# FFN token columns at a stride of 124, and a down product with 128 stationary columns

## The chip, the cores and the metric

The kernel runs on one core of a Trainium2 chip. The metric is the device time of one execution in microseconds, lower is better. A slot and a sample, used below, are units of the kernel's own loop.

## What is computed

The input is x of 64 x 55 x 55 x 96 floats. First a depthwise convolution with 25 x 25 taps of which every third counts, multiplied by x, plus a bias, plus x. The result is taken as 64 samples of 3025 tokens of 96 channels. A token mixer follows: layer norm, a product to 192 channels with ReLU, a Fourier transform over the tokens, gates on the real and the imaginary part, the inverse transform, and a product back to 96 channels, added to the tokens. Last comes the FFN, the part that the change touches:

```python
def _qlinear(x, W, b):
    y = q_acc(jnp.einsum('bsk,nk->bsn', q_mul(x), q_mul(W)))
    return q_acc(y + q_mul(b))
...
h = jax.nn.relu(_qlinear(x, W1, b1))      # 96 -> 384
y = _qlinear(h, W2, b2)                   # 384 -> 96
...
t = t + _L1_ffn_ref(_ln_t(t), W1, b1, W2, b2)
```

`q_mul` rounds to an 8-bit float with 5 exponent and 2 mantissa bits, `q_acc` to a 16-bit float with 5 and 10.

## The kernel before

There are two stages. `conv_stage` (lines 170 to 344) does the convolution and writes to DRAM. `mixer_stage` (from line 347) first sets up weights and constants in a block of its own (lines 440 to 567, with the clearing of buffers at lines 540 to 546), and then runs everything else as one software pipeline.

The 3025 tokens of a sample are 121 x 25: 121 (`U`) on the partitions, 25 (`S`) columns. A sample is cut into eight chunks of columns, the first of 4 and seven of 3 (`CHUNK`). So there are 512 chunks, and the pipeline's loop counter g, a slot, runs from -9 to 555. In each slot every engine does one piece of each step, each for another chunk: a step with offset k works on chunk g - k. The order in a slot is written out by hand, one loop to an engine (TensorE lines 1137 to 1161, ScalarE 855 to 881, VectorE 990 to 1010, GpSimd 750 to 759, the DMA queue of SyncE 693 to 710), and semaphores connect them.

TensorE in slot g: `columns` (line 1021, the second forward transform), `rows` part 1 (1046), `widen` part 0 (1033), `mix` (1061, 1062), `rows` part 0 (1046), `inverse` (1073), `down` (1085), `turn` (1098), `widen` part 1 (1033), `inverse_rows` (1122), `up` (1111), `turn2` (1133). `rows` part 1 waits, through the bank that they share, for VectorE's `residual` (line 985, writes `t2`), which waits for the `inverse_rows` of the slot before.

The FFN of a chunk with w columns (3 or 4) goes through these steps:

- `normalise` (VectorE, 961) writes the normalised tokens in fp8 and `turn2` turns them, with an output of 121 columns for each token column, 128 apart in PSUM
- `out_turn2` (ScalarE, 768) copies them to `xq`, fp8, 96 partitions, with the token columns side by side at a stride of 121
- `up` (TensorE, offset 41): three matmuls (`FM` = 3) with `w1q` stationary, 128 columns, and `xq` moving, 121 w columns, into three banks
- `out_up` (ScalarE, 838) copies the three to `y16`, f16, rows of 484
- `widen_bias` (VectorE, offset 42): three additions of the bias with ReLU on `y16` in place (921), of 121 w elements rounded up to even, and one cast to `hq` in fp8 (927)
- `down` (TensorE, offset 42, same slot): for each token column and each m of three, one load of 121 columns of `hq` as the stationary operand and one matmul with `w2q` moving, 96 columns: 3 w pairs of load and matmul
- `out_down` (ScalarE, 821) and `finish` (GpSimd, 733 and 737): copy, bias, residual, then the DMA to `out`

GpSimd's five operations of a slot are `cut_value` (721), `add_sum` (727), `scale` (747) and `finish` (733, 737); ahead of them it waits for this slot's `normalise`. In slots with g modulo 8 equal to 6, VectorE first computes the layer norms' `variance` (lines 896 to 902) of a whole sample, before `residual`, and at its end `inverse_root` (908 to 912). In slots 1 to 5 it does the statistics of five incoming columns (969).

Of the kernel before, what the change touches and what calls it, by code (L numbers as in the profile page):

```python
# [11 lines left out]
F8 = mybir.dt.float8e5  # L12
# [3 lines left out]
C = 96  # L16
# [3 lines left out]
FM = F // 128  # L20
# [59 lines left out]
U = 121  # L80
# [12 lines left out]
PART = (0, 5, 10, 15, 20, 25)  # L93
JC = 4
KC = 8
TOK = JC * U
AR = 3
XR = 3
OR = 3
# [18 lines left out]
def tokens(n):  # L118
    return CHUNK[n % NS], CHUNK[n % NS + 1]
# [15 lines left out]
def upto(n):  # L135
    return max(0, min(n, CHUNKS))
# [210 lines left out]
def mixer_stage(nc, x1, p, a_d, g_d, out):  # L347
    with ExitStack() as ctx:
        def sb(name, shape, dt=F32):
            return ctx.enter_context(nc.sbuf_tensor(name, shape, dt))  # L350
# [18 lines left out]
        w2q = sb("w2q", [128, FM, C], F8)  # L369
# [20 lines left out]
        xn2 = [sb(f"xn2{s}", [U, JC, C], F8) for s in range(2)]  # L390
        xq = [sb(f"xq{s}", [C, TOK], F8) for s in range(XR)]
        y16 = [sb(f"y16{s}", [128, FM, TOK], F16) for s in range(2)]
        hq = [sb(f"hq{s}", [128, FM, TOK], F8) for s in range(2)]
        z16 = [sb(f"z16{s}", [U, JC, C], F16) for s in range(2)]
        o_sb = [sb(f"o_sb{s}", [U, JC, C]) for s in range(OR)]
        bn = sb("bn", [U, 2 * S, 6])
# [6 lines left out]
        ps = ctx.enter_context(nc.psum_tensor("ps", [128, 8, 512], F32))  # L403


        with ExitStack() as wctx:
# [69 lines left out]
            def _(dve):  # L476
                steps = [0]

                def then(ins):

                    steps[0] += 1
                    ins.then_inc(w_step, 1)
                    dve.wait_ge(w_step, steps[0])

                dve.wait_ge(w_in, 16 * (LOADS - 1))
                last = None
# [5 lines left out]
                for v, n in zip((var1, var2, rows[3], rows2[3]), newton):  # L492
                    last = nc.vector.reciprocal(v, n[1])
                then(last)
                for v, n in zip((var1, var2, rows[3], rows2[3]), newton):
                    last = nc.vector.tensor_tensor(n[1], v, v, ALU.mult)
                then(last)
                for v, n in zip((var1, var2, rows[3], rows2[3]), newton):
                    last = nc.vector.tensor_tensor(n[1], n[1], n[0], ALU.mult)
                then(last)  # L500
                for v, n in zip((var1, var2, rows[3], rows2[3]), newton):
                    last = nc.vector.tensor_scalar(n[1], n[1], -0.5, 1.5, ALU.mult, ALU.add)
                then(last)
                for v, n in zip((var1, var2, rows[3], rows2[3]), newton):
                    last = nc.vector.tensor_tensor(v, v, n[1], ALU.mult)
# [11 lines left out]
                for a in range(2):  # L517
                    last = nc.vector.tensor_scalar(w1n[:, a, :], w1n[:, a, :], gam1[:, a:a + 1], None,
                                                   ALU.subtract)
# [20 lines left out]
                nc.vector.memset(mixed[:, PAIRS_K, :], 0.0)  # L540
                for v in toks:
                    nc.vector.memset(v[:, :, C:C + 1], 1.0)
                for v in y16:
                    nc.vector.memset(v[:, :, :], 0.0)
                then(nc.vector.memset(spec[HH:HH + 1, :, :, :], 0.0))
                nc.vector.memset(spec[HH:HH + 1, 0, 0, 0:1], 1.0)

# [72 lines left out]
        TURNED, WIDE, ROW, MIXP, INVP, DOWNP = 2, 3, 4, 5, 6, 7  # L620
# [141 lines left out]
        def _(act):  # L762
            def out_turn2(n):
                w = tokens(n)[1] - tokens(n)[0]
                act.wait_ge(turned2, n + 1)
                if n >= XR:
                    act.wait_ge(f1_done, n - XR + 1)
                nc.scalar.activation(xq[n % XR][:, 0:w * U].rearrange("p (j t) -> p j t", t=U),
                                     ps[0:C, TURNED, :].rearrange("p (j t) -> p j t", j=JC)[:, 0:w, 0:U],
                                     ACT.Copy, saturate=False).then_inc(xq_ready, 1)  # L770

# [59 lines left out]
                                     ACT.Copy).then_inc(xnt_ready, 1)  # L831

            def out_up(n):
                w = (tokens(n)[1] - tokens(n)[0]) * U
                act.wait_ge(f1_done, n + 1)
                if n >= 2:
                    act.wait_ge(hq_ready, n - 1)
                nc.scalar.activation(y16[n % 2][:, :, 0:w], ps[:, MIXP:MIXP + FM, 0:w],  # L838
                                     ACT.Copy).then_inc(y16_ready, 1)
# [15 lines left out]
            for g in SLOTS_G:  # L855
                if here(g - TURN2 - 1):
                    out_turn2(g - TURN2 - 1)
                if here(g - GATE):
                    gate_value(g - GATE)
                if here(g - 1):  # L860
                    rows_out(g - 1, 1)
                if here(g):
                    relu(g, 0)
                if here(g - GATE):
                    gate_sum(g - GATE)
                if g % NS == 6 and 0 <= (g + 2) // NS < B + 5:
                    root((g + 2) // NS)
                if here(g - MIX):
                    out_mix(g - MIX)
                if here(g):  # L870
                    rows_out(g, 0)
                if here(g - INV):
                    out_inverse(g - INV)
                if here(g - DOWN):
                    out_down(g - DOWN)
                if here(g - TURN):
                    out_turn(g - TURN)
                if here(g):
                    relu(g, 1)
                if here(g - UP):  # L880
                    out_up(g - UP)

        @block.vector
        def _(dve):
# [28 lines left out]
                dve.sem_inc(scale_ready, 1)  # L913

            def widen_bias(n):
                w = (tokens(n)[1] - tokens(n)[0]) * U
                w += w % 2
                y, q = y16[n % 2], hq[n % 2]
                dve.wait_ge(y16_ready, n + 1)
                for m in range(FM):  # L920
                    last = nc.vector.tensor_scalar(y[:, m, 0:w], y[:, m, 0:w], b1q[:, m:m + 1], 0.0,  # L921
                                                   ALU.add, ALU.max)
                last.then_inc(relu_ready, 1)
                if n >= 2:
                    dve.wait_ge(f2_done, n - 1)
                dve.wait_ge(relu_ready, n + 1)
                nc.vector.tensor_copy(q[:, :, 0:w], y[:, :, 0:w], saturate=False).then_inc(hq_ready, 1)  # L927
# [85 lines left out]
        def _(pe):  # L1013
            def columns(t):
                p0, _, n, hf = group(t)
                pe.wait_ge(acol_in[t % NS // 2], 16 * (t // NS + 1))
                if t:
                    pe.wait_ge(v_ready, t)
                    pe.wait_ge(m_ready, t)
                for p in range(n):  # L1020
                    last = nc.tensor.matmul(COL[:, p, 0:Q], acol[:, p0 + p, hf * HH:(hf + 1) * HH],  # L1021
                                            fb[:, p0 + p, :], start=True, stop=True)
                last.then_inc(x_done, 1)
# [53 lines left out]
            def down(n):  # L1077
                w = tokens(n)[1] - tokens(n)[0]
                pe.wait_ge(hq_ready, n + 1)
                pe.wait_ge(y16_ready, n + 1)  # L1080
                if n:
                    pe.wait_ge(z_ready, n)
                for j in range(w):
                    for m in range(FM):
                        last = nc.tensor.matmul(ps[0:U, DOWNP, C * j:C * (j + 1)],  # L1085
                                                hq[n % 2][:, m, j * U:(j + 1) * U], w2q[:, m, :],
                                                start=(m == 0), stop=(m == FM - 1))
                last.then_inc(f2_done, 1)

# [10 lines left out]
                last.then_inc(turned, 1)  # L1100

            def up(n):
                w = (tokens(n)[1] - tokens(n)[0]) * U
                pe.wait_ge(xq_ready, n + 1)
                pe.wait_ge(w2_ready, upto(n + UP - MIX + 1))
                pe.wait_ge(g_ready, upto(n + UP - INV + 1))
                if n:
                    pe.wait_ge(z_ready, n)
                    pe.wait_ge(y16_ready, n)
                for m in range(FM):  # L1110
                    last = nc.tensor.matmul(ps[:, MIXP + m, 0:w], w1q[:, m * 128:(m + 1) * 128],  # L1111
                                            xq[n % XR][:, 0:w], start=True, stop=True)
                last.then_inc(f1_done, 1)
# [59 lines left out]
def build(nc, p, out):  # L1173
    x1 = nc.dram_tensor("x1_d", [E, B, R * R, EC], F32).ap()
    a_d = nc.dram_tensor("a_d", [B, S, M, H], F32).ap()
    g_d = nc.dram_tensor("g_d", [B, S, M, C], F32).ap()
    conv_stage(nc, p["items"], p["bands"], p["cb"], p["c_id"], x1)
    mixer_stage(nc, x1, p, a_d, g_d, out)
# [22 lines left out]
```

## Time and profile before

| | |
|---|---|
| median of 3 runs | 5087.42 us (5086.44 to 5088.37) |
| span of the profiled execution | 5082.0 us |
| convolution, then set-up | until 896 us |
| pipeline in its steady state | 1237 to 4790 us |
| tail, after the last chunks enter | 4790 to 5082 us |

The page gives for each engine its busy time over the span, and the span in 40 slices with the busy share in tenths:

```profile
PE 4747.4 (93%) x40842; PEld 4227.9 (83%) x40842; DVE 3785.3 (74%) x10870; ACT 3808.6 (75%) x7819; POOL 2488.9 (49%) x2603
...
PE   8999994699999999999999999999999999999974
PEld 7888884488888888888888888888888888888853
DVE  3444443247888888888888888888888888888884
ACT  3444442378888888888888888888888888888853
POOL 2335432144555555555555555555555555555542
PEclk9999997599999999999999999999999999999985
```

PE is TensorE's matmuls, PEld its weight loads (which overlap the matmuls), DVE is VectorE, ACT ScalarE, POOL GpSimd. Matmuls are pipelined and their durations overlap, so the time that a run of them takes is read from the chain of work, which counts each moment once, and not from the sum of durations. PEclk is the granted clock of TensorE; a value of 1.00 in a table is the full 2.4 GHz.

### The profile page before, as it was taken

What the parts mean: (1) busy time and instruction counts of PE and PEld (TensorE: products, weight loads), DVE (VectorE), ACT (ScalarE), POOL (GpSimd) and SP (SyncE); (2) the same over time, 40 slices, a digit from 0 to 9 for tenths busy, and PEclk for the clock granted to TensorE, in tenths of its full rate; (3) what the DMA queues carried; (4) which work ended last, traced back from release to release, by engine and by line L of the source; (5) the groups of instructions that cost most, each with busy time, mean ns of one, the idle gap of its engine ahead of it and who ended that gap; (6) DMA issues with size and microseconds to landing.
All of it is one profiled execution on the core that took longest, in us unless ns stands there. A gap on an engine that the chain in (4) does not pass through costs nothing.

```text
span 5082.0 us, 121784 instructions
## 1 busy us (share of the span) xinstructions
PE 4747.4 (93%) x40842; PEld 4227.9 (83%) x40842; DVE 3785.3 (74%) x10870; ACT 3808.6 (75%) x7819; POOL 2488.9 (49%) x2603
## 2 busy tenths in 40 slices
PE   8999994699999999999999999999999999999974
PEld 7888884488888888888888888888888888888853
DVE  3444443247888888888888888888888888888884
ACT  3444442378888888888888888888888888888853
POOL 2335432144555555555555555555555555555542
PEclk9999997599999999999999999999999999999985
DMA  6777775256666666666666666666666666666541
GB/s 204 246 226 242 239 234 153 81 161 179 174 180 175 172 176 177 178 176 177 177 174 176 178 176 179 177 179 175 179 173 174 178 176 179 176 177 175 156 115 30
DMA packets 781423, 893.15 MB, mean 176 GB/s; under 512 B 236243, under 2 KB 689292, under 8 KB 768652
## 3 DMA queue, kind: packets, MB, share of 16 engines
q1 hardware_dynamic: 780556, 885.27, 63.5%
q8 instruction: 347, 5.69, 0.5%
q14 instruction: 256, 2.10, 0.1%
q10 hardware_dynamic: 264, 0.10, 0.0%
HBM read 500.64 MB, written 384.61 MB: 174 GB/s over the span
## 4 chain that ended last, share of the span: by engine, by line
PE 68%; DVE 8%; ACT 3%; issue 3%; DMA 0%; POOL 0%; DVEq 0%; POOLq 0%
PE ps L1021 12%; PE ps L1046 10%; PE ps L1033 10%; PE ps L1062 6%; PE ps L1061 6%; PE ps L1073 6%; PE ps L1085 5%; PE ps L1111 4%; PE ps L1122 4%; PE ps L1098 3%; PE ps L1133 1%; ACT ps L791 1%; DVE gv L946 1%; ACT spec L786 1%; DVE mean L896 1%
## 5 line engine op out<-in xcount | busy, mean ns | idle before, releaser
L721 POOL TENSOR_SCALAR gv<-gv 96x400 f32<-96x400 f32 (+1 forms) x512 | 599.6, 1171 | 1675.8 <-DVE xn L961 1587.6
L838 ACT ACTIVATE y<-ps 128x1089 f16<-128x1089 f32 (+1 forms) x512 | 572.9, 1119 | 328.7 <-PE ps L1111 328.7
L340 PE MATMUL cps<-toep,xin 114*128 114x190 f32 (+2 forms) x3456 | 775.9, 339 | 44.2 <-issue 25.5
L1046 PE MATMUL ps<-hid,fa 121*128 121x384 f32 (+1 forms) x2048 | 734.1, 441 | 82.9 <-DVE t L985 70.6
L1021 PE MATMUL ps<-fb,acol 100*96 100x100 f32 x7936 | 786.5, 252 | 15.0 <-DVE spec L953 14.5
L1021 PEld LDWEIGHTS ps<-fb,acol 100*96 100x96 f32 x7936 | 724.9, 164 | 25.3 <-issue 25.0
L286 ACT ACTIVATE xo<-cps 128x180 f32<-128x180 f32 (+3 forms) x576 | 367.4, 638 | 451.0 <-PE cps L343 451.0
L317 DVE SCALAR_TENSOR_TENSOR xo<-cps,xo 128x180 f32<-128x180 f32 (+3 forms) x576 | 362.7, 630 | 459.2 <-ACT xo L286 458.7
L1033 PE MATMUL ps<-w1t,xnt 97*121 97x192 f32 x3200 | 702.9, 330 | 0.7 <-ACT xnt L829 0.7
L1061 PE MATMUL ps<-w2t,spec 97*100 97x96 f32 x3968 | 673.2, 252 | 4.7 <-ACT y L838 4.7
L1062 PE MATMUL ps<-w2t,spec 96*100 96x96 f32 x3968 | 675.8, 252 | 0.0
L340 PEld LDWEIGHTS cps<-toep,xin 114*128 114x128 f32 x3456 | 531.0, 194 | 108.4 <-issue 31.1
L295 POOL TENSOR_TENSOR xo<-xo,conv_cbias 128x3960 f32<-128x3960 f32 (+1 forms) x39 | 317.6, 8169 | 514.5 <-DVE xo L317 514.5
L921 DVE TENSOR_SCALAR y<-y,b1q 128x364 f16<-128x364 f16 (+1 forms) x1536 | 486.0, 371 | 107.2 <-ACT y L838 106.9
L1061 PEld LDWEIGHTS ps<-w2t,spec 97*100 97x100 f32 x3968 | 546.7, 168 | 5.2 <-POOL spec L727 2.7
L1073 PEld LDWEIGHTS ps<-mixed,ib 100*100 100x100 f32 x3968 | 430.5, 168 | 144.2 <-issue 78.5
L1033 PEld LDWEIGHTS ps<-w1t,xnt 97*121 97x121 f32 x3200 | 526.6, 188 | 19.0 <-issue 1.2
L927 DVE CAST hq<-y 128x1092 fp8e5<-128x1092 f16 (+1 forms) x512 | 470.1, 918 | 54.4 <-DVE y L921 2.3
L1062 PEld LDWEIGHTS ps<-w2t,spec 96*100 96x100 f32 x3968 | 510.5, 168 | 0.0
L799 ACT ACTIVATE hid<-ps 121x384 f32<-121x384 f32 (+1 forms) x1024 | 431.5, 421 | 98.4 <-PE ps L1033 66.0
L943 DVE SCALAR_TENSOR_TENSOR spec<-ps,rd,gq 96x400 f32<-96x400 f32 (+1 forms) x512 | 314.6, 614 | 251.4 <-ACT ps L791 251.2
L852 ACT ACTIVATE arow<-ps 128x384 f32<-128x384 f32 (+1 forms) x1024 | 426.7, 417 | 93.2 <-PE ps L1046 91.0
(105 smaller groups left out, 10581.5 us busy)
## 6 DMA issues: line engine op xcount, KB each, us to landing
a_d<-arow SPq DMA_DIRECT2D x448, 288.0 KB, 3.9
acol<-a_d SPq DMA_DIRECT2D x192, 600.0 KB
xin<-in_items SPq DMA_DIRECT2D x96, 1008.0 KB
g_d<-mixed SPq DMA_DIRECT2D x256, 300.0 KB
tok<-x_d SPq DMA_DIRECT2D x64, 1134.4 KB
out<-o_sb SPq DMA_DIRECT2D x448, 136.1 KB
x_d<-xo SPq DMA_DIRECT2D x48, 990.0 KB, 11.9
grow<-g_d SPq DMA_DIRECT2D x128, 312.0 KB, 11.2
```

The costliest lines, as they stand in the source:

```text
L340: last = nc.tensor.matmul(ps[2 * (m % DEEP)][:, (r0 - o0) * GC:(r1 - o0) * GC], xb, toep[e % 2][0:GP, c, at * GC:(at + r1 - r0) * GC], sta ...
L721: nc.gpsimd.tensor_scalar(v, v, 0.0, None, ALU.max).then_inc(v_cut, 1)
L799: nc.scalar.activation(hid[part][:, 0:s1 - s0, :].rearrange("p j h -> p (j h)"), ps[0:U, WIDE, 0:(s1 - s0) * H], ACT.Relu).then_inc(hid_re ...
L838: nc.scalar.activation(y16[n % 2][:, :, 0:w], ps[:, MIXP:MIXP + FM, 0:w], ACT.Copy).then_inc(y16_ready, 1)
L921: last = nc.vector.tensor_scalar(y[:, m, 0:w], y[:, m, 0:w], b1q[:, m:m + 1], 0.0, ALU.add, ALU.max)
L927: nc.vector.tensor_copy(q[:, :, 0:w], y[:, :, 0:w], saturate=False).then_inc(hq_ready, 1)
L1021: last = nc.tensor.matmul(COL[:, p, 0:Q], acol[:, p0 + p, hf * HH:(hf + 1) * HH], fb[:, p0 + p, :], start=True, stop=True)
L1033: last = nc.tensor.matmul(ps[0:U, WIDE, j * H:(j + 1) * H], xnt[n % 2][:, s0 - c0 + j, :], w1t[:, :], start=True, stop=True)
L1046: nc.tensor.matmul(ps[0:M, ROW, 0:(s1 - s0) * H], fa[:, :], hid[part][:, 0:s1 - s0, :].rearrange("p j h -> p (j h)"), start=True, stop=Tru ...
L1061: nc.tensor.matmul(o, spec[0:HH + 1, 0, p, :], w2t[0:HH + 1, 0, :], start=True, stop=False)
L1062: last = nc.tensor.matmul(o, spec[0:HH, 1, p, :], w2t[0:HH, 1, :], start=False, stop=True)
L1073: last = nc.tensor.matmul(ps[0:Q, INVP, (p - p0) * C:(p - p0 + 1) * C], ib[:, p, :], mixed[:, p, :], start=True, stop=True)
```

## The change

The token columns of a chunk lie 124 apart in `xq`, `y16` and `hq` in place of 121, so each begins at a multiple of four bytes in fp8. `up`, `out_up`, `widen_bias` and the cast work on 124 w columns (372 or 496 in place of 363 or 484), so the gaps of three are computed along, and need no further rounding to even. `down` loads 128 columns from each start, the last seven of them from the gap and the next token column (or, at the end, from four further elements by which the rows of `hq` are made longer), and writes 128 partitions of PSUM, of which `out_down` reads 121 as before. `xq` and `hq` are cleared in the set-up as `y16` was.

```diff
--- before.py
+++ after.py
@@ -93,7 +93,8 @@
 PART = (0, 5, 10, 15, 20, 25)
 JC = 4
 KC = 8
-TOK = JC * U
+UP4 = 124
+TOK = JC * UP4
 AR = 3
 XR = 3
 OR = 3
@@ -390,7 +391,7 @@
         xn2 = [sb(f"xn2{s}", [U, JC, C], F8) for s in range(2)]
         xq = [sb(f"xq{s}", [C, TOK], F8) for s in range(XR)]
         y16 = [sb(f"y16{s}", [128, FM, TOK], F16) for s in range(2)]
-        hq = [sb(f"hq{s}", [128, FM, TOK], F8) for s in range(2)]
+        hq = [sb(f"hq{s}", [128, FM, TOK + 4], F8) for s in range(2)]
         z16 = [sb(f"z16{s}", [U, JC, C], F16) for s in range(2)]
         o_sb = [sb(f"o_sb{s}", [U, JC, C]) for s in range(OR)]
         bn = sb("bn", [U, 2 * S, 6])
@@ -540,8 +541,10 @@
                 nc.vector.memset(mixed[:, PAIRS_K, :], 0.0)
                 for v in toks:
                     nc.vector.memset(v[:, :, C:C + 1], 1.0)
-                for v in y16:
+                for v in (*y16, *hq):
                     nc.vector.memset(v[:, :, :], 0.0)
+                for v in xq:
+                    nc.vector.memset(v[:, :], 0.0)
                 then(nc.vector.memset(spec[HH:HH + 1, :, :, :], 0.0))
                 nc.vector.memset(spec[HH:HH + 1, 0, 0, 0:1], 1.0)
 
@@ -765,7 +768,7 @@
                 act.wait_ge(turned2, n + 1)
                 if n >= XR:
                     act.wait_ge(f1_done, n - XR + 1)
-                nc.scalar.activation(xq[n % XR][:, 0:w * U].rearrange("p (j t) -> p j t", t=U),
+                nc.scalar.activation(xq[n % XR][:, :].rearrange("p (j t) -> p j t", t=UP4)[:, 0:w, 0:U],
                                      ps[0:C, TURNED, :].rearrange("p (j t) -> p j t", j=JC)[:, 0:w, 0:U],
                                      ACT.Copy, saturate=False).then_inc(xq_ready, 1)
 
@@ -831,7 +834,7 @@
                                      ACT.Copy).then_inc(xnt_ready, 1)
 
             def out_up(n):
-                w = (tokens(n)[1] - tokens(n)[0]) * U
+                w = (tokens(n)[1] - tokens(n)[0]) * UP4
                 act.wait_ge(f1_done, n + 1)
                 if n >= 2:
                     act.wait_ge(hq_ready, n - 1)
@@ -913,8 +916,7 @@
                 dve.sem_inc(scale_ready, 1)
 
             def widen_bias(n):
-                w = (tokens(n)[1] - tokens(n)[0]) * U
-                w += w % 2
+                w = (tokens(n)[1] - tokens(n)[0]) * UP4
                 y, q = y16[n % 2], hq[n % 2]
                 dve.wait_ge(y16_ready, n + 1)
                 for m in range(FM):
@@ -1082,8 +1084,8 @@
                     pe.wait_ge(z_ready, n)
                 for j in range(w):
                     for m in range(FM):
-                        last = nc.tensor.matmul(ps[0:U, DOWNP, C * j:C * (j + 1)],
-                                                hq[n % 2][:, m, j * U:(j + 1) * U], w2q[:, m, :],
+                        last = nc.tensor.matmul(ps[:, DOWNP, C * j:C * (j + 1)],
+                                                hq[n % 2][:, m, j * UP4:j * UP4 + 128], w2q[:, m, :],
                                                 start=(m == 0), stop=(m == FM - 1))
                 last.then_inc(f2_done, 1)
 
@@ -1100,7 +1102,7 @@
                 last.then_inc(turned, 1)
 
             def up(n):
-                w = (tokens(n)[1] - tokens(n)[0]) * U
+                w = (tokens(n)[1] - tokens(n)[0]) * UP4
                 pe.wait_ge(xq_ready, n + 1)
                 pe.wait_ge(w2_ready, upto(n + UP - MIX + 1))
                 pe.wait_ge(g_ready, upto(n + UP - INV + 1))
```

## Rows read from the trace of the kernel before

**Rows 1.** Busy time by stretch: us, engines, granted clock, DMA share, GB/s.

```profile
1237.00:4790.00 3553.00, 3487.67 (x32100) 3149.29 (x32099) 3046.16 (x9142) 3090.80 (x6511) 1950.53 (x2307) 1.00 0.66 176
```

**Rows 2.** The chain of work over one sample, 3000 to 3061.64 us, by line.

```profile
by line: PE ps L1021 15.4%; PE ps L1046 13.2%; PE ps L1033 12.7%; PE ps L1062 8.0%; PE ps L1061 8.0%; PE ps L1073 7.7%; PE ps L1085 6.0%; PE ps L1111 5.5%; PE ps L1122 5.5%; PE ps L1098 4.2%; issue 2.4%; PE ps L1133 1.9%; DVE mean L896 1.3%
```

**Rows 3.** Timeline of GpSimd: start us, us, instruction, idle before and its releaser.

```profile
3025.81 0.83 POOL L747 TENSOR_TENSOR toks<-tok,rstd 121x384 f32<-121x384 f32 x1 [0.92 <-DVEq L913]
...
3087.45 0.82 POOL L747 TENSOR_TENSOR toks<-tok,rstd 121x384 f32<-121x384 f32 x1 [0.92 <-DVEq L913]
```

**Rows 4.** The chain in order of time, 3008 to 3027 us: start us, us, what.

```profile
3009.18 0.16 PE ps L1133 x3
...
3017.22 0.62 DVE mean L899
...
3018.45 0.57 DVE t L985
3019.02 0.14 issue
3019.16 0.56 PE ps L1046 x2
...
3022.98 0.49 PE ps L1085 x9
...
3026.68 0.41 PE ps L1046 x2
```

**Rows 5.** Timeline of VectorE and TensorE where slot 7 begins.

```profile
3025.91 0.46 DVE L985 TENSOR_TENSOR t<-ps,t_res 121x288 f32<-121x288 f32 x1 [0.24 <-DVE rstd L912]
...
3026.52 0.56 PE L1046 MATMUL ps<-hid,fa 121*128 121x192 f32 x2
```

**Rows 6.** The chain in order of time in slot 2, 3045 to 3056 us.

```profile
3053.57 0.66 PE ps L1085 x12
```

**Rows 7.** Groups by line and form, 1300 to 5000 us: busy us, mean ns, idle before.

```profile
L1085 PEld LDWEIGHTS ps<-w2q,hq 128*121 128x121 fp8e5 x4557 | 313.8, 139 | 46.5 <-DVE hq L927 46.3
L1111 PEld LDWEIGHTS ps<-xq,w1q 96*128 96x128 fp8e5 x1457 | 140.3, 97 | 155.0 <-issue 32.4
L838 ACT ACTIVATE y<-ps 128x1089 f16<-128x1089 f32 x424 | 458.6, 1082 | 254.2 <-PE ps L1111 254.2
L927 DVE CAST hq<-y 128x1092 fp8e5<-128x1092 f16 x425 | 390.3, 918 | 45.6 <-DVE y L921 2.3
L927 DVE CAST hq<-y 128x1452 fp8e5<-128x1452 f16 x61 | 56.0, 918 | 6.2
L953 DVE TENSOR_TENSOR spec<-ps,spec 96x400 f32<-96x400 f32 x349 | 195.3, 560 | 0.0
L953 DVE TENSOR_TENSOR spec<-ps,spec 96x350 f32<-96x350 f32 x118 | 59.9, 507 | 0.0
```

**Rows 8.** Waits, 1237 to 4790 us: who for whom, us in total, times, longest.

```profile
ACT y L838 <- PE ps L1111: 268.7, 461, 0.7
DVE t L985 <- PE ps L1122: 239.2, 290, 1.2
```

**Rows 9.** Timeline of GpSimd and VectorE: end of slot 5, slots 7, 2 and 3.

```profile
3017.00 0.79 POOL L737 TENSOR_TENSOR o_sb<-t,z 121x288 f32<-121x288 f32 x1
...
3026.91 1.45 DVE L921 TENSOR_SCALAR y<-y,b1q 128x364 f16<-128x364 f16 x3
...
3050.63 0.92 DVE L927 CAST hq<-y 128x1452 fp8e5<-128x1452 f16 x1
...
3052.93 0.63 DVE L943 SCALAR_TENSOR_TENSOR spec<-ps,rd,gq 96x400 f32<-96x400 f32 x1 [0.24 <-ACT ps L791]
...
3055.44 0.46 DVE L985 TENSOR_TENSOR t<-ps,t_res 121x288 f32<-121x288 f32 x1 [0.85 <-PE ps L1122]
...
3057.10 0.75 DVE L921 TENSOR_SCALAR y<-y,b1q 128x364 f16<-128x364 f16 x3
```

**Rows 10.** Line 544, the clearing of `y16`: duration ns min/median/max, first and last start.

```profile
L544 DVE MEMSET y<- x2: 663/663/663, 887.7 to 888.5; 128x726 uint32 x2
```

**Rows 11.** The chain in order of time in the tail, 5034 to 5056 us.

```profile
5040.70 1.18 PE ps L1085 x9
```

## The prediction

> **What bounds the kernel now.** I read the busy shares and the clock by stretch first [rows 1]. From 1237 to 4790 us the granted clock is 1.00 (2.4 GHz) and TensorE is busy for 3488 of 3553 us; the change touches this stretch, a short tail behind it and a little set-up. A busy share names only a suspect, so I went on to the chain of work, by line, over one sample [rows 2]. A sample is eight slots; GpSimd's line 747 has its four-column form once in each, 61.64 us apart [rows 3]. TensorE's lines carry nearly all of the chain, line 1085 (down) 6.0% of it and line 1111 (up) 5.5%. I name a slot by g modulo 8.
>
> The chain in order of time shows the exception [rows 4]. From 3026.68 on it stays on TensorE for 46.7 us, until slot 5 of the next sample. There, at the time that answers to 3011.76, the widening matmuls are done and the chain goes through ScalarE's gates to VectorE: the gates, the variance (line 899 in it), `t` at 3018.45, and only then TensorE's line 1046 at 3019.16. Slot 7 is a near tie: VectorE's next `t` ends at 3025.91 + 0.46 = 3026.37, and TensorE's line 1046 begins at 3026.52 [rows 5], 0.15 us after it, as it does after the `t` that ends at 3019.02. So VectorE sets the end of slots 5 and 6, and what TensorE saves in these two is lost. What it saves in slots 7, 0, 1, 2, 3 and 4 counts.
>
> **Down, per pair.** Nine pairs take 0.49 us [rows 4], twelve 0.66 [rows 6]: 54.7 ns each, with 121 columns loaded and 96 streamed. The pairs of line 1133 load 96 and stream 121, and take 0.16/3 = 53.3 ns [rows 4]. So the longer operand seems to set the spacing. A streamed column costs 0.417 ns at the full clock of this stretch. If the load became short, a down pair would be bound by its 96 columns: 53.3 - 25 x 0.417 = 42.9 ns. Does it become short? The load of 121 one-byte columns takes 139 ns, that of 128 columns in line 1111 only 97 [rows 7]: seven columns more, 42 ns less. Its start is a multiple of 128 bytes; that a multiple of four suffices no row shows. I take the short load: 11.8 ns a pair saved. The six counted slots hold 5 x 9 + 12 = 57 pairs: 0.67 us.
>
> The Trainium skill, "TensorE: Matmul & The Clock Gate", section "Weight-path perf modes — Fast Weight Load (FWL) and DoubleRow", says that loads of exactly 128 non-FP32 weights are read 32 bits at a time; the 97 ns row agrees. Its section "Back-to-back issue gap" gives about 81 ns for a sustained pair of load and matmul at 128 columns, by which down would gain nothing; the rows at 53.3 and 54.7 ns already contradict it.
>
> **Up.** 9 more moving columns (12 in the four-column chunk) in three matmuls each: 0.011 or 0.015 us, in the six slots 0.07 us lost. ScalarE's copy of the result grows from 1089 to 1116 elements, at 1082/1089 ns an element [rows 7] 27 ns. It is hidden: ScalarE waits for up in 461 slots, 0.58 us on average [rows 8]; without that cover it would cost 27 ns a slot. The copy to `xq` writes as many elements as before, with a stride: nothing.
>
> **VectorE, three-column chunks.** Three bias additions of 372 in place of 364 elements cost between nothing and 8 x 1.06 ns each (slope of line 953 from 350 to 400 elements, 507 to 560 ns [rows 7]); I take 10 ns together. The cast has 24 elements more at 918/1092 ns [rows 7]: 20 ns. These 30 ns are on the path twice a sample: slot 6 lies in it, and slot 5's cast leads to GpSimd's work, beside which the variance runs. Line 899 ends at 3017.84 [rows 4], just after GpSimd's line 737 at 3017.79 [rows 9], so GpSimd seems to hold it up. 0.06 us lost.
>
> **VectorE, the four-column chunk: a hidden cost.** Before, the rows of `y16` and of `hq` touch (484 of 484), so the cast of 1452 elements is one run; it takes 918 ns, as three rows of 364 do [rows 7]. After, the rows of `hq` are 500 apart and hold 496, while `y16` is one run of 1488. Bounds: by the row form 1488 x 918/1092 = 1251 ns (+0.33 us); by line 953's 1.06 ns an element and its remainder of 136 ns, 1713 ns (+0.79). A gain is excluded: more elements in a looser layout. I take +0.79, the worse for the forecast.
>
> The Trainium skill, "VectorE: DVE Perf Modes", section "What auto-detection actually checks", wants the outermost dimensions of source and destination both even or equal for the two-port mode; 1488 against 3 fails it, so by it the slow end holds. That two shapes so unlike take the same 918 ns agrees with the rule.
>
> The delay falls in slot 2. There VectorE next waits 0.24 us for ScalarE and then 0.85 us for TensorE [rows 9]; 0.79 + 0.13 of TensorE's own gain is below 1.09. TensorE's down wants `hq` at 3053.57 [rows 6]; the cast ended at 3051.55 [rows 9], now 3052.34. Queued behind the cast are join and normalise, and behind normalise GpSimd's five operations, which begin 0.79 us later and run into slot 3's bias additions. These took 1.45 us where GpSimd ran beside them (slot 7) and 0.75 where not [rows 9], so slot 3 may lose 0.5 us more. VectorE's wait for TensorE, 0.82 us on average in 290 slots [rows 8], holds that; by slot 5 I expect the delay gone. Cost nothing.
>
> **The sum.** Per sample 0.67 - 0.07 - 0.06 = 0.54 us; 3553/61.64 = 57.6 samples: 31.3 us. Set-up: clearing 726 words takes 663 ns [rows 10]; `hq` adds 2 x 375 words and `xq` 3 x 124, about 1.2 us with an instruction's fixed part, all in line. Tail: some 40 slots with everything in series and TensorE slower, nine pairs in 1.18 us [rows 11], which is 121 columns at 1.2 GHz and a rest. Bound by 96 columns they save 25 x 0.83 = 20 ns each; less up, ScalarE and VectorE (0.08), 0.1 us a slot, and 0.4 us lost in each of five wide slots: 2 us gained. Total 31.3 - 1.2 + 2 = 32 us. The profiled span is 5082.0 and the median 5087.42, some 5 us around the span; 5087.4 - 32 = 5055.
>
> **Rivals.** (A) A pair has a floor of its own: no row shows a spacing below 53.3 ns. Then 57 x 1.4 = 0.08 us less the 0.13 lost, +3 us with 57.6 samples, and the set-up: 5091. Against it: the 121 streamed columns explain 53.3. Chance 0.12. (B) The load isn't shortened, as `hq`'s starts are multiples of four bytes only, so the change doesn't do what it says: seven more columns, 2.9 x 57 = 0.17, and 0.13: 0.30 a sample, 17 us, 5105. Chance 0.06. (C) Slower by VectorE and GpSimd: the cast's delay doesn't fade, reaches slot 5 through GpSimd and lengthens the variance. It decides from the point where slot 2's delay passes 1.09 us, or GpSimd's end in slot 4 passes the start of slot 5's additions. All of it costs 0.79 - 0.54 = 0.25 us a sample, 5102; half of it 5079. For: TensorE's gain takes 0.1 us a slot off that slack. Against: the waits above. Chance 0.08, half of it slower. (D) Better than the sum (40 ns a pair, fewer collisions with GpSimd): 5035 to 5044, 0.04.
>
> **How the numbers follow.** The forecast case has 0.70 and its own range of 5044 to 5066: a pair between 40 and 45 ns (9 and 7 us) and 3 us in the tail. With (A), half of (C) and the edge of (D) it is 5042 to 5091. A measurement tells about 0.2% (10 us) from no change. Faster: 0.70 + 0.04 and 0.03 of (C), 0.77. Same: (A) and 0.01 of (C), 0.13. Slower: (B) and 0.04, 0.10.
>
> **What the profile after would show.** Loads of line 1085 near 97 ns; nine pairs in 0.39 us of the chain; slots 0, 1, 3 and 4 some 0.1 us shorter, 5 and 6 not; the cast of 1488 near 1.7 us; TensorE's one wait for `t` in a sample longer by 0.1 to 0.3 us. It would be wrong if loads stay at 139 ns or more (B), if they are short and pairs stay at 53 (A), or if the additions of slots 3 to 5 take 1.4 us (C).

## The result, and the profile after

The changed kernel takes 5051.9 us (median; 5039.2 to 5054.0), the kernel before beside it 5087.9: a ratio of 0.993, with an interval of 0.991 to 0.994. The forecast was 5055 in a range of 5042 to 5091. The medians differ by 36.0 us; the profiled span falls from 5082.0 to 5052.2 us, by 29.8. The length of the convolution and of the first fill varies from run to run by some 20 us, whatever the change: the four-column form of GpSimd's line 747 that opens the steady state starts between 1219 and 1240 us in the ten traces. So for the causes I compare the time of one sample in the steady state, which repeats within 0.02 us in all but four or five of the 57 samples of each of these two traces (those take up to 0.4 us more).

The timeline of GpSimd gives it as before [rows 3]; line 747 is now 750, and for all lines here the numbers are 2 or 3 higher:

```profile
3011.72 0.83 POOL L750 TENSOR_TENSOR toks<-tok,rstd 121x384 f32<-121x384 f32 x1 [0.92 <-DVEq L916]
...
3072.86 0.83 POOL L750 TENSOR_TENSOR toks<-tok,rstd 121x384 f32<-121x384 f32 x1 [0.92 <-DVEq L916]
```

This sample takes 61.14 us (median over the run 61.16) in place of 61.64: 0.48 us less, by 57.6 samples 28 us. The same instruction at both ends of the steady state gives 3515.1 us before (1237.46 to 4752.59) and 3486.9 after, 28.3 less. From there to the end it is 329.4 and 327.7, 1.6 less, and up to there nothing. Only the first of these three is beyond chance: with a start that varies by 20 us, and an end that is 322.1 and 328.6 us long in two of the kernels below that differ in one cast alone, the other two show nothing.

Groups by line and form, 1300 to 4950 us (busy us, mean ns, idle before), which answer to [rows 7]:

```profile
L1087 PEld LDWEIGHTS ps<-w2q,hq 128*128 128x128 fp8e5 x4518 | 242.8, 99 | 38.7 <-DVE hq L929 38.3
L1135 PEld LDWEIGHTS ps<-ident,xn 121*96 121x96 fp8e5 x1507 | 150.4, 124 | 54.3 <-issue 2.1
L1048 PEld LDWEIGHTS ps<-hid,fa 121*128 121x128 f32 x1828 | 276.1, 190 | 92.7 <-issue 87.2
L923 DVE TENSOR_SCALAR y<-y,b1q 128x372 f16<-128x372 f16 x1269 | 499.8, 448 | 38.8 <-ACT y L841 38.6
L841 ACT ACTIVATE y<-ps 128x1116 f16<-128x1116 f32 x422 | 464.7, 1101 | 241.8 <-PE ps L1113 241.8
L929 DVE CAST hq<-y 128x1116 fp8e5<-128x1116 f16 x422 | 394.0, 934 | 44.2 <-DVE y L923 0.9
L929 DVE CAST hq<-y 128x1488 fp8e5<-128x1488 f16 x60 | 102.2, 1703 | 6.5 <-DVE y L923 0.5
```

The loads of down take 99 ns where they took 139. Two other loads in the list set limits to that: 96 fp8 columns take 124 ns (line 1135), and 128 columns of f32 take 190 (line 1048), so in these rows neither fewer columns nor a count of 128 in f32 gives the short load. The casts take 934 and 1703 ns; the second is the hidden cost of the forecast. The additions of the bias take 448 ns, far more than eight elements explain; before, in the same window, they took 378:

```profile
L921 DVE TENSOR_SCALAR y<-y,b1q 128x364 f16<-128x364 f16 x1254 | 405.7, 378 | 38.3 <-ACT y L838 38.2
```

The chain in order of time, 2985 to 3050 us, which answers to [rows 4, 6]:

```profile
2992.92 0.38 PE ps L1087 x9
...
3001.32 0.90 DVE mean L899
...
3004.35 0.57 DVE t L987
...
3005.06 0.56 PE ps L1048 x2
...
3012.47 0.52 PE ps L1048 x2
...
3039.19 0.51 PE ps L1087 x12
```

Nine pairs take 0.38 us in place of 0.49, twelve 0.51 in place of 0.66: 42.3 ns a pair. Line 1048 in slot 7 (3012.47) now takes 0.52 us of the chain where it took 0.41, since TensorE gets there 0.1 us earlier and still waits for `t`. The start of `inverse_rows` in each slot shows where the 0.49 us went (us from one to the next; slot 5 is from slot 4's to its own):

| slot | 5 | 6 | 7 | 0 | 1 | 2 | 3 | 4 |
|---|---|---|---|---|---|---|---|---|
| before | 7.13 | 8.80 | 7.65 | 7.63 | 7.68 | 7.80 | 7.48 | 7.48 |
| after | 7.03 | 8.93 | 7.66 | 7.53 | 7.58 | 7.67 | 7.38 | 7.38 |

Each slot whose end TensorE sets is 0.10 us shorter (0.13 with four columns). Slot 5's 0.10 comes back in slot 6 with 0.03 on top, and slot 7 gains nothing from one such start to the next: its own down saves 0.11 us, but the 0.11 us that slot 6's down saved only lengthens the wait for `t` ahead of it.

The timeline of VectorE shows what the slow cast did to the three slots after it (slots 2, 3, 4 and 5):

```profile
3036.28 1.70 DVE L929 CAST hq<-y 128x1488 fp8e5<-128x1488 f16 x1
3040.90 0.46 DVE L987 TENSOR_TENSOR t<-ps,t_res 121x288 f32<-121x288 f32 x1 [0.20 <-PE ps L1124]
3042.56 1.41 DVE L923 TENSOR_SCALAR y<-y,b1q 128x372 f16<-128x372 f16 x3
...
3049.94 1.11 DVE L923 TENSOR_SCALAR y<-y,b1q 128x372 f16<-128x372 f16 x3
...
3057.32 0.86 DVE L923 TENSOR_SCALAR y<-y,b1q 128x372 f16<-128x372 f16 x3
```

VectorE still waits 0.20 us for TensorE in slot 3, so slot 2 holds the 0.79 us. But GpSimd began its five operations later and stood in the additions of the next slots, which took 1.41, 1.11 and 0.86 us in place of 0.75. Its last operation in each of the three slots, in the timeline of GpSimd:

```profile
3042.71 0.92 POOL L740 TENSOR_TENSOR o_sb<-t,z 121x384 f32<-121x384 f32 x1
...
3049.76 0.73 POOL L740 TENSOR_TENSOR o_sb<-t,z 121x288 f32<-121x288 f32 x1
...
3056.89 0.73 POOL L740 TENSOR_TENSOR o_sb<-t,z 121x288 f32<-121x288 f32 x1
```

It ends 1.07, 0.55 and 0.30 us after the additions began, and they are 0.66, 0.36 and 0.11 us longer than the plain 0.75. In the kernel before the same operation ends 0.08 us after slot 3's additions begin, and these take 0.75. That GpSimd is the carrier is read from these rows; no run took its work away. In slot 5, 0.11 us is left of the delay.

### The profile page after: what moved, and what is told of

The parts are those of the page before. It is cut to its first block, busy times and chain, and to the rows that moved or that the text cites. A ratio compares the mean times of both kernels' runs of the same rounds, so it can differ in the third digit from the quotient of the medians.

```text
span 5052.2 us, 121789 instructions
## 1 busy us (share of the span) xinstructions
PE 4694.7 (93%) x40842; PEld 4162.8 (82%) x40842; DVE 3932.6 (78%) x10875; ACT 3791.2 (75%) x7819; POOL 2489.8 (49%) x2603
## 4 chain that ended last, share of the span: by engine, by line
PE 67%; DVE 8%; ACT 3%; issue 3%; DMA 0%; POOL 0%; DVEq 0%; POOLq 0%; ACTq 0%
PE ps L1023 12%; PE ps L1048 10%; PE ps L1035 10%; PE ps L1064 6%; PE ps L1063 6%; PE ps L1075 6%; PE ps L1113 5%; PE ps L1124 4%; PE ps L1087 4%; PE ps L1100 3%; PE ps L1135 1%; DVE mean L899 1%; ACT ps L794 1%; DVE gv L948 1%; ACT spec L789 1%
## 5 line engine op out<-in xcount | busy, mean ns | idle before, releaser
L841 ACT ACTIVATE y<-ps 128x1116 f16<-128x1116 f32 (+1 forms) x512 | 583.7, 1140 | 319.8 <-PE ps L1113 319.8
L923 DVE TENSOR_SCALAR y<-y,b1q 128x372 f16<-128x372 f16 (+1 forms) x1536 | 579.3, 431 | 103.5 <-ACT y L841 103.2
L929 DVE CAST hq<-y 128x1116 fp8e5<-128x1116 f16 (+1 forms) x512 | 527.3, 1030 | 53.7 <-DVE y L923 1.4
L730 POOL TENSOR_TENSOR spec<-spec,gc 96x400 f32<-96x400 f32 (+1 forms) x512 | 484.7, 947 | 0.0
```

The lines of the kernel that those rows point to most:

```text
L730: nc.gpsimd.tensor_tensor(sv, sv, gc[t % 2][:, 0:n, :], ALU.add).then_inc(s_ready, 1)
```

## The experiments

Every kernel is one edit of the changed kernel or of the one before; the code cuts show the lines that matter, with `...` for what is left out. The table gives a sample's time as the median over the run, and the median time of the kernel beside that of the kernel before on the same chip.

| kernel | a sample, us | time, us | before, us | ratio, interval |
|---|---|---|---|---|
| before | 61.64 | 5087.9 | | |
| changed | 61.16 | 5051.9 | 5087.9 | 0.993 (0.991 to 0.994) |
| rows of `hq` touch | 61.03 | 5038.0 | 5084.3 | 0.992 (0.989 to 0.994) |
| down loads 121 | 61.76 | 5100.3 | 5084.3 | 1.004 (1.002 to 1.005) |
| 128 at a stride of 121 | 60.93 | 5032.0 | 5084.3 | 0.990 (0.988 to 0.993) |
| only `hq` at 124 | 60.93 | 5024.2 | 5084.3 | 0.989 (0.986 to 0.993) |
| 121 in slots 5 and 6 | 61.15 | 5058.8 | 5085.1 | 0.995 (0.993 to 0.997) |
| 64 columns streamed | 61.55 (best 60.73) | 5094.0, one run | 5085.1 | |
| slow cast in slot 5 | 61.38 (64.4 at worst) | 5097.0, one run | 5085.1 | |
| slow cast in slot 1 | 60.93 | 5024.7, one run | 5085.1 | |

**Is it the number of columns or where they begin?** Two kernels, one that takes the 128 columns away and keeps the starts, and one that does the reverse.

```diff
-  last = nc.tensor.matmul(ps[:, DOWNP, C * j:C * (j + 1)], hq[n % 2][:, m, j * UP4:j * UP4 + 128], ...
+  last = nc.tensor.matmul(ps[0:U, DOWNP, C * j:C * (j + 1)], hq[n % 2][:, m, j * UP4:j * UP4 + U], ...
```

> The changed kernel, in which down loads 121 columns again, from the same starts at multiples of four bytes. My theory (the number of columns makes the load short, and the load sets a pair's spacing): loads go back from 99 to 139 ns, nine pairs from 0.38 to 0.49 us, a sample gains 57 x 0.0125 = 0.71 us to about 61.8, and the time is 5088 to 5095, no better than before the change. Rival (the starts do it): loads near 99 ns, time near 5052.

```diff
-  hq = [sb(f"hq{s}", [128, FM, TOK], F8) for s in range(2)]
+  hq = [sb(f"hq{s}", [128, FM * TOK + 8], F8) for s in range(2)]
...
+  at = m * TOK + j * U
-  last = nc.tensor.matmul(ps[0:U, ...], hq[n % 2][:, m, j * U:(j + 1) * U], ...
+  last = nc.tensor.matmul(ps[:, ...], hq[n % 2][:, at:at + 128], ...
```

> The kernel before, in which down loads 128 columns from starts at the old stride of 121, three in four of them no multiple of four bytes; hq is one piece with 8 elements more. Theory (the count alone decides): loads near 97 ns, nine pairs in 0.38 us, none of the costs of the wider stride: a sample of 61.64 - 0.71 = 60.93 us, time about 5046. Rival (the starts matter): loads at 139 ns or more, pairs 2.9 ns longer than before, a sample of 61.8, time near 5098; or a mix, if the aligned quarter alone is short.

Groups by form, first of the kernel that loads 121 columns from the new starts, then of the one that loads 128 from the old:

```profile
L1087 PEld LDWEIGHTS ps<-w2q,hq 128*121 128x121 fp8e5 x4470 | 308.4, 139 | 26.5 <-DVE hq L929 26.1
```

```profile
L1089 PEld LDWEIGHTS ps<-w2q,hq 128*128 128x128 fp8e5 x4539 | 244.6, 99 | 42.0 <-DVE hq L929 41.8
```

For these fp8 loads the number of columns decides and the start doesn't: 139 ns for 121 columns from aligned starts, 99 for 128 from starts of which three in four are no multiple of four bytes. Counts between 121 and 128 weren't run. The second kernel reaches 60.93 us a sample, exactly what the 57 pairs give with no cost beside. So the wider stride, by which `xq`, `y16` and all the work on them grew, bought nothing here. Loading 121 columns leaves its costs: 61.76, slower than before. That is 0.60 us above the changed kernel, and 57 pairs at 12.4 ns would be 0.71. The other 0.11 is in slot 5's additions, which in this kernel take the plain time again (timeline of VectorE, slots 4 and 5), as slower slots let the slow cast's delay fade in time:

```profile
2988.09 1.01 DVE L923 TENSOR_SCALAR y<-y,b1q 128x372 f16<-128x372 f16 x3
...
2995.58 0.75 DVE L923 TENSOR_SCALAR y<-y,b1q 128x372 f16<-128x372 f16 x3
```

**Do slots 5 and 6 count?**

```diff
+  c = U if (n + DOWN) % NS in (5, 6) else 128
-  ... ps[:, ...], hq[n % 2][:, m, j * UP4:j * UP4 + 128] ...
+  ... ps[0:c, ...], hq[n % 2][:, m, j * UP4:j * UP4 + c] ...
```

> The changed kernel, in which down loads 121 columns again in slots 5 and 6 alone and 128 in the other six. My theory (VectorE sets the end of these two slots): the 18 slow pairs, 0.22 us, are covered; TensorE's waits for t shrink by as much, and a sample stays at 61.16 us, the time near 5052. Rival (all eight slots count): the sample grows by 18 x 0.0125 = 0.22 us to 61.38 and the time by 13 us.

In the chain in order of time nine pairs of slot 6 are slow again, and the wait in slot 7 shrinks by what they lose:

```profile
3002.83 0.56 PE ps L1048 x2
3005.45 0.67 PE ps L1048 x2
3006.65 0.50 PE ps L1088 x9
3010.36 0.41 PE ps L1048 x2
```

A sample takes 61.15 us, as with all slots short. Two of eight slots are worth nothing. The profiled span is 5052.1 against 5052.2; the times of this kernel, 5058.8 in the median, lie over a spread of 30 us and can't tell 7 us.

**Is the slow cast what lengthens the additions, and what does it cost?** `hq` in one piece with touching rows of 496; its clearing, the cast and down address the new shape, and nothing else changed.

```diff
-  hq = [sb(f"hq{s}", [128, FM, TOK + 4], F8) for s in range(2)]
+  hq = [sb(f"hq{s}", [128, FM * TOK + 4], F8) for s in range(2)]
...
+  at = m * TOK + j * UP4
-  ... hq[n % 2][:, m, j * UP4:j * UP4 + 128] ...
+  ... hq[n % 2][:, at:at + 128] ...
```

> The changed kernel with the rows of hq touching again (1492 elements in one piece, rows of 496), so that the four-column cast is one run of 1488. My theory: that cast falls from 1703 ns to about 935, nothing is late in slot 2, and the bias additions of slots 3, 4 and 5, which took 1.41, 1.11 and 0.87 us, go back to 0.75. The 0.12 us that slot 5's additions lost stood ahead of GpSimd's work and the variance, so a sample falls from 61.16 to 61.04 us and the time by 7 us, to about 5045. Rival: the additions are longer because their rows are now 372 elements at other starts; then they stay at 0.9 to 1.4 us and the sample at 61.16.

Timeline of VectorE in slots 3, 4 and 5 of a sample:

```profile
2917.66 0.85 DVE L925 TENSOR_SCALAR y<-y,b1q 128x372 f16<-128x372 f16 x3
...
2925.04 0.75 DVE L925 TENSOR_SCALAR y<-y,b1q 128x372 f16<-128x372 f16 x3
...
2932.42 0.76 DVE L925 TENSOR_SCALAR y<-y,b1q 128x372 f16<-128x372 f16 x3
```

The additions of slots 4 and 5 are short again with rows of 372, slot 3's take 0.85 us, the cast of 1488 elements takes 935 ns, and a sample falls by 0.13 us to 61.03. The cost of the cast's 0.77 us is thus 0.12 to 0.13 us a sample, the part still there in slot 5. Over all slots an addition takes 402 ns here, against 378 before the change. Most of that rest isn't the rows of 372: it is 394 ns in the kernel with 128 columns at a stride of 121, whose rows are 364 as before.

**Where does a slow cast cost?** In the kernel with 128 columns at a stride of 121, the cast of one chunk in eight writes one run of 1089 from three rows of 363, once for slot 5's chunk and once for slot 1's.

```diff
+  if n % NS == 3:      # slot 5; 7 for slot 1
+      nc.vector.tensor_copy(q[:, 0:FM * 3 * U], y[:, :, 0:3 * U], saturate=False).then_inc(hq_ready, 1)
+      return
...
+  at = m * (3 * U if n % NS == 3 else TOK) + j * U
```

> The kernel before with 128 columns loaded at a stride of 121 (60.93 us a sample), in which the chunk of slot 5 is cast from three rows of 363 into one run of 1089, outermost counts 3 and 1089. Theory: by odd and unequal counts the cast runs at one element a step, 1.29 us in place of 0.92; slot 5's cast stands ahead of GpSimd's work and the variance, so all of the 0.37 us reaches the sample: 61.30. Rival (VectorE's wait for ScalarE in that slot, 0.4 to 0.5 us, absorbs it): 60.93.

> The same slow cast in slot 1 in place of slot 5. Theory: the delay of 0.37 us pushes GpSimd into the additions of slots 2 and 3, shrinks by 0.25 to 0.3 us a slot as it did in the changed kernel (0.66, 0.37, 0.12 us in slots 3, 4, 5), and is gone by slot 5: a sample of 60.93 us. Rival (a delay of VectorE costs wherever it falls): 61.30.

By the groups both casts took 1292 ns. In slot 1 it costs nothing: 60.93, and slot 2's additions took 0.86 us as without it, so the delay was gone in the very next slot, a step earlier than I had said. In slot 5 a sample takes 61.31 to 61.39 where the clock is 1.00, 0.38 to 0.46 above 60.93, or 0.01 to 0.09 more than the cast's own 0.37. In these two places, at least, place decides, as stated. But a part of its samples takes 62 to 64.4 us, which no theory had. The table of stretches over such a sample's slots 5 and 6 shows why (columns as in [rows 1]; the third number from the end is the granted clock):

```profile
3759.00:3761.00 2.00, 0.82 (x10) 0.66 (x8) 1.86 (x7) 1.41 (x3) 0.98 (x2) 1.00 0.86 153
3761.00:3763.00 2.00, 1.57 (x9) 1.56 (x9) 1.86 (x9) 0.42 (x2) 0.00 (x0) 0.82 0.81 156
3763.00:3765.00 2.00, 2.00 (x15) 2.00 (x13) 1.94 (x5) 2.00 (x5) 0.00 (x0) 0.50 0.94 247
3765.00:3767.00 2.00, 2.00 (x9) 1.35 (x8) 1.97 (x4) 0.75 (x3) 1.97 (x2) 0.50 0.78 232
3767.00:3769.00 2.00, 2.00 (x18) 1.99 (x17) 0.88 (x5) 1.19 (x3) 0.98 (x2) 0.50 0.74 146
3769.00:3771.00 2.00, 2.00 (x18) 1.65 (x17) 0.86 (x4) 1.15 (x4) 1.46 (x2) 0.97 0.74 153
```

TensorE waited 1.61 us for `t` until 3761.43. Then the clock stood at half, 1.2 GHz, until about 3769, and the sample took 3 us longer. In other samples the same wait of 1.61 us left the clock alone.

**Has a pair a floor of its own?** Down streams 64 of 96 columns.

```diff
-  ps[:, DOWNP, C * j:C * (j + 1)], ..., w2q[:, m, :]
+  ps[:, DOWNP, C * j:C * j + 64], ..., w2q[:, m, 0:64]
```

> The changed kernel, in which down streams 64 of the 96 columns of w2q (a third of the FFN's output channels is left out). Theory (with a short load the streamed columns set the spacing): a pair takes 42.4 - 32 x 0.417 = 29 ns, nine pairs 0.26 us, and a sample falls by up to 57 x 0.0133 = 0.76 us to 60.4 to 60.6. Rival (a pair has a floor of its own near 40 ns, by its load or its issue): nine pairs stay at 0.36 to 0.38 us and the sample at 61.1.

The chain in order of time, one group of nine:

```profile
2059.33 0.26 PE ps L1087 x9
```

A pair takes 29 ns: the streamed columns set it, and the load of 128 columns no longer does. The sample missed its mark. At best it takes 60.73 to 60.81 us (five samples, the clock at 1.00 in each), 0.35 to 0.43 below the changed kernel and not 0.76. In one of them (2047 to 2108 us) the additions of slots 3 to 5 took 1.44, 1.25 and 1.12 us, so three times as much of the slow cast's delay is left in slot 5: shorter slots leave it less room to fade. That is 0.26 us of the 0.33 to 0.41 missing; the rest is open. TensorE's wait for `t` was 1.78 us there, and many samples have a granted clock below 1.00 (0.97 from 1300 to 1426 us). From 2978 to 4392 us a sample takes 61.3 to 61.7 us, more than half of them 61.42 to 61.46, and there, in the stretch shown, one with a dip of the clock comes before one without:

```profile
3040.13:3101.57 61.44, 59.58 (x548) 53.45 (x547) 56.21 (x159) 52.49 (x113) 34.15 (x40) 0.97 0.68 179
3101.57:3163.03 61.46, 59.75 (x572) 53.75 (x571) 55.45 (x159) 53.79 (x114) 33.84 (x40) 1.00 0.65 176
```

The dip stands in slot 6, right behind the wait: TensorE's wait ends at 3094.29, and the clock is at 0.5 from 3095 to 3098 us. It falls so near the end of its sample that the next one can inherit part of the loss. The two together take 1.28 us more than two of 60.81, and 0.03 of 61.44 us is 1.8 us of full clock. So the dips are enough to explain both; no run shows it by itself.

**The version without the costs.** `xq` and `y16` stay as before the change; the cast alone spreads the token columns to 124.

```diff
+  nc.vector.tensor_copy(q[:, 0:FM * JC * UP4].rearrange("p (m j t) -> p m j t", m=FM, j=JC)[:, :, 0:k, 0:U],
+      y[:, :, 0:k * U].rearrange("p m (j t) -> p m j t", t=U), saturate=False).then_inc(hq_ready, 1)
...
+  at = (m * JC + j) * UP4
```

> Only hq has its token columns at 124: xq, y16, up, ScalarE's copy and the additions stay at 121 columns as before, and the cast spreads them (runs of 121 at a stride of 124, hq in one piece). Theory: short loads as in the changed kernel, and no cost for up (0.07), for 30 ns of VectorE twice, nor for the slow cast (0.12): a sample near 61.64 - 0.71 = 60.93 us, time about 5042 to 5046, better than the changed kernel. Rival: writing in runs of 121 slows the cast to over 1.1 us; then the 0.2 us comes twice a sample and the time is 5055 to 5065.

Its two casts, by form:

```profile
L931 DVE CAST hq<-y 128x1089 fp8e5<-128x1089 f16 x424 | 390.5, 921 | 45.5 <-DVE y L924 2.3
L931 DVE CAST hq<-y 128x1452 fp8e5<-128x1452 f16 x61 | 56.1, 920 | 6.3
```

Writing in runs of 121 costs 2 to 3 ns. A sample takes 60.93 us, 0.71 less than before and 0.23 less than with the change as it was made. Its median is the lowest, 5024.2 us, a ratio of 0.989, but its runs (5013 to 5043 us) overlap those of the kernel that loads 128 columns at a stride of 121 (5023 to 5040). In the steady state the two are level, and that other one needs the smaller edit.

## Why the prediction was right, and where it was off

- **The load and the pair.** A load near 97 ns and a pair of 42.9 ns were forecast, 99 and 42.3 measured. That 121 loaded columns had set the spacing, and not a floor, is shown by the 29 ns with 64 streamed. Rivals (A) and (B) fall. The question that I had left open, whether starts at multiples of four bytes suffice, has the answer that they do, and that they aren't needed either. The rule of the Trainium skill that I had cited (TensorE: Matmul & The Clock Gate, "Weight-path perf modes — Fast Weight Load (FWL) and DoubleRow"), 128 weights that aren't FP32, holds at all four remainders of the address; its 81 ns a pair, from "Back-to-back issue gap", isn't seen in the fp8 pairs of these traces, which take 29 to 54.7 ns at the full clock (none streams 128 columns).
- **57 of 75 pairs count.** Slots 5 and 6 are worth nothing, shown by undoing them alone. Both kernels without other costs gained 0.71 us a sample; the step had 0.67, and with the measured 12.4 ns a pair it is 0.71.
- **Up and the three-column chunks.** 0.13 us was forecast. The kernel with touching rows (61.03) and the one at a stride of 121 (60.93) differ by these costs alone: 0.10.
- **The slow cast.** Its size was right, 1703 ns against 1713, though the rows of before gave only bounds, 1251 and 1713, and the upper one was taken as the worse. "Cost nothing" was the step that failed. The forecast had up to 0.5 us more in slot 3's additions and nothing left in slot 5; it was 0.66, 0.36 and 0.11 us in slots 3, 4 and 5. It costs 0.12 to 0.13 us a sample, 7 us: slot 5's cast stands ahead of GpSimd's work and the variance, where a delay counts, as the slow cast placed there showed. This was rival (C) with a sixth of its price. The rule that I had set against the change (VectorE: DVE Perf Modes, "What auto-detection actually checks") is borne out: 1488 against 3 rows gives the slow form, and 1089 against 3 as well (1292 ns).
- **The sum.** 0.54 us a sample was forecast, 0.48 measured: 0.71 - 0.10 - 0.13. Up to the steady state I had 1.2 us lost; `hq`'s and `xq`'s clearing take 0.77 and 0.43 us in the timeline, as said, but the same point of the steady state came only 0.1 us later. The tail gave 1.6 us of the 2 forecast. Both are within what varies from run to run, so that the total agrees so well, 30 of 32 us in spans and 36 in medians, is luck in these two terms; what repeats is the steady state, 28.3 us of the 31.3 forecast. The tail's working was off as well: where nine pairs had taken 1.18 us they now take 0.91, 30 ns a pair less and not 20, and from 4850 to 4925 us the granted clock of before was still 0.93, so not all of the 40 slots ran at 1.2 GHz.
- **A slip in the last step.** I took 5 us to lie around the span, from a span of 5082.0 and a median of 5087.42. The changed kernel's profiled run shows 5054.0 with a span of 5052.2, so only 1.8 lie around it, and the profiled run of before lay some 3.6 us below its median. It didn't hurt, since only the difference was used.
- **What no rival had:** the clock. Making TensorE faster makes its wait for `t` longer (1.13 us before, 1.36 after, 1.6 to 1.8 in two experiments). In the changed kernel the clock stayed at 1.00 even after waits of 1.67 and 1.68 us. In those two experiments it fell in many samples, and in three others (touching rows, 128 at a stride of 121, only `hq` at 124), whose usual wait is 1.23 us, once each, behind a longer one of 1.53, 1.60 and 1.58 us.

## What to carry to other kernels

For fp8 operands, load exactly 128 stationary columns even if fewer are needed, and let the last ones fall on whatever lies behind: down's pair is then bound by what it streams. Change the layout only where the step reads or writes it, and time every copy whose source becomes one run while its destination doesn't: one run into three rows was slow, one run into twelve wasn't. Before adding up savings, find the slots that another engine ends, and follow a delay of VectorE through GpSimd into the slots after it.

## What the runs showed of the hardware that I had not expected

- Short fp8 loads need no aligned start: 99 ns at a stride of 121 bytes, as at 124.
- The clock can fall in the middle of a steady state in which TensorE is busy to 98%: after an idle stretch of 1.61 us it stood at 1.2 GHz for some 7 us, in some samples and not in others. The kernel before, with its usual wait of 1.13 us and its longest of 1.47, has no sample above 62.01 us and a clock of 1.00. The version without the costs has one at 62.40, with a granted clock of 0.86 and 0.71 in two stretches of 4 us, right behind a wait of 1.58 us.
- A cast between shapes as unlike as one run of 1452 and twelve runs of 121 keeps its speed (920 ns); one between three rows and one run doesn't.
